# A post-norm decoder layer on one core: 1/std of the second and third layer norm from Ln and Exp on ScalarE and one refinement step on VectorE, in place of a bit-trick guess and three Newton steps on GpSimd

## What is computed

```
def _layernorm(x, axis=-1, eps=1e-05):
    m = jnp.mean(x, axis=axis, keepdims=True)
    v = jnp.var(x, axis=axis, keepdims=True)
    return (x - m) / jnp.sqrt(v + eps)

x = _layernorm(x + gelu((x @ ((w1 @ w2.T) * sparse_mask)) + b2))
x = _layernorm(x + cross_attention(x, ctx, ctx, mask, wq, wk, wv, wo))   # 32 query heads, 8 key heads, rope, softmax over 64 keys
x = _layernorm(x + x @ W.T + b + 2 * sum_e routing[b, e] * (x @ A_e.T) @ B_e.T)   # routing: softmax of the mean over tokens 107..254
```

## Time and profile before

| what | value |
|---|---|
| median of 3 runs | 492.2 us (491.89 to 492.32) |
| the profiled execution | 492.99 us, span 491.2 us |
| mean granted TensorE clock | 0.985 |
| busy share of the span | PE 96%, VectorE 83%, GpSimd 56%, ScalarE 53% |
| chain that ended last | PE 77%, VectorE 9%, the SP queue 4%, GpSimd 3%, issue 3%, DMA 2%, ScalarE 1% |

### The profile page before, as it was taken

One profiled execution on the slowest core, in us unless ns is written; L12 is line 12 of the kernel. 1 busy time (PEld: TensorE's weight loads), 2 busy tenths in 40 slices (PEclk: granted clock), 3 DMA queues, 4 the chain that ended last, 5 costly groups with the idle time before them and its releaser, 6 DMA issues.

```text
span 491.2 us, 11126 instructions
## 1 busy us (share of the span) xinstructions
PE 473.9 (96%) x4189; PEld 395.9 (81%) x4189; DVE 408.3 (83%) x739; ACT 260.6 (53%) x462; POOL 273.4 (56%) x347
## 2 busy tenths in 40 slices
PE   8999999999999999999999999999999999879991
PEld 8888778888888888888888888888888788668781
DVE  2779898988987898798979987988799889988585
ACT  4574447735673566365735663575458254353423
POOL 3477637854674467456636672676366423156523
PEclk9999999999999999999999999999999999979996
DMA  8943300240023011402040212022002400000013
GB/s 274 353 146 93 124 1 1 87 130 1 2 85 128 0 22 63 128 0 80 7 127 0 85 34 94 0 85 85 0 0 87 67 1 2 1 0 2 0 40 133
DMA packets 29137, 31.56 MB, mean 64 GB/s; under 512 B 6321, under 2 KB 16817, under 8 KB 29114
## 3 DMA queue, kind: packets, MB, share of 16 engines
q1 hardware_dynamic: 29114, 31.25, 20.1%
HBM read 29.15 MB, written 2.10 MB: 64 GB/s over the span
## 4 chain that ended last, share of the span: by engine, by line
PE 77%; DVE 9%; SPq 4%; POOL 3%; issue 3%; DMA 2%; ACT 1%; ACTq 0%; POOLq 0%; DVEq 0%
PE bank L261 23%; PE bank L263 22%; PE bank L262 22%; PE bank L369 6%; PE bank L393 3%; SPq L205 2%; DMA WQr<-in_L_xattn_wq_dram 2%; DVE X L1223 1%; DVE BST L1187 1%; PE bank L267 1%; POOL NW L1711 1%; DVE VWl L1139 1%; POOL NW L1709 1%; POOL RS L1713 1%; POOL NW L1707 1%
## 5 line engine op out<-in xcount | busy, mean ns | idle before, releaser
L1722 POOL TENSOR_TENSOR QS<-QS,SIN 128x512 f32<-128x512 f32 x64 | 83.0, 1297 | 124.4 <-ACT QS L801 124.4
L261 PE MATMUL bank<-XTh,WQh 128*128 128x512 f32 x256 | 101.7, 397 | 0.7 <-DVE XTl L1139 0.7
L263 PE MATMUL bank<-XTh,WQl 128*128 128x512 f32 x256 | 100.0, 391 | 0.0
L262 PE MATMUL bank<-XTl,WQh 128*128 128x512 f32 x256 | 99.7, 390 | 0.0
L1139 DVE TENSOR_TENSOR VWl<-bank,VWh 64x512 fp32r<-64x512 f32 x128 | 88.0, 688 | 9.3 <-ACT VWh L801 7.4
L801 ACT ACTIVATE QS<-bank 128x512 f32<-128x512 f32 x64 | 38.3, 598 | 103.1 <-PE bank L263 102.6
L801 ACT ACTIVATE VWh<-bank 64x512 fp32r<-64x512 f32 x128 | 75.9, 593 | 23.5 <-PE bank L263 20.9
L1251 DVE TENSOR_TENSOR bank<-bank,COS 128x512 f32<-128x512 f32 x64 | 44.6, 697 | 23.2 <-ACT QS L801 22.6
L261 PEld LDWEIGHTS bank<-XTh,WQh 128*128 128x128 f32 x256 | 48.1, 188 | 11.5 <-issue 1.3
L263 PEld LDWEIGHTS bank<-XTh,WQl 128*128 128x128 f32 x256 | 48.0, 188 | 10.5
L262 PEld LDWEIGHTS bank<-XTl,WQh 128*128 128x128 f32 x256 | 48.1, 188 | 9.5
(11 more groups left out here) (150 smaller groups left out, 965.1 us busy)
## 6 DMA issues: line engine op xcount, KB each, us to landing
WQr<-in_L_xattn_wq_dram SPq DMA_DIRECT2D x8, 1024.0 KB, 5.5
WOr<-in_L_xattn_wo_dram SPq DMA_DIRECT2D x8, 1024.0 KB, 5.4
KVr<-in_L_xattn_wk_dram SPq DMA_DIRECT2D x8, 256.0 KB, 5.4
KVr<-in_L_xattn_wv_dram SPq DMA_DIRECT2D x8, 256.0 KB, 5.5
out_dram<-X SPq DMA_DIRECT2D x8, 256.0 KB, 2.0
X<-in_x_dram SPq DMA_DIRECT2D x3, 512.0 KB, 9.9
WQr<-in_L_attn_w_dram SPq DMA_DIRECT2D x4, 256.0 KB, 4.9
WOr<-in_L_attn_w_dram SPq DMA_DIRECT2D x4, 256.0 KB, 5.1
```

The costliest lines, as they stand in the source:

```text
L261: pe.matmul(o, lh, rh, start=start, stop=False)
L262: pe.matmul(o, lh, rl, start=False, stop=False)
L263: return pe.matmul(o, ll, rh, start=False, stop=stop)
L1722: pool.tensor_tensor(q, q, SIN[:, :].unsqueeze(1).broadcast_to([P, 2, S]), ALU.mult)\
```

## The change

For layer norms 1 and 2, `guess`, `newton`, `mean_shift` and `out_last` are no longer called. In their place ScalarE's `std_first` writes Exp(-0.5 * Ln(var + eps)) of a pair, in two dependent activations on 128x2. VectorE's `std_step` then does one Newton step in three dependent fused instructions, and a fourth for minus mean times 1/std. The last pair goes the same way, with tile 6 written by VectorE (`out_by_dve`) as before. GpSimd sets the tile `EPS` once at the start and has no part in these two norms any more. Layer norm 0 is as it was.

With it, the written order of all four engines from group LAST on is another one, and so are some bank tables (`x2_bank`, `fy_bank`, `F_BANKS`, `LORA_BANKS`, `ROUTE_BANK`). The number of matmuls and the loop over the groups before LAST are the same.

```
+            def std_first(k, m):
+                pair, n = slice(2 * m, 2 * m + 2), 4 * (k - 1) + m
+                act.wait_ge(sm["ln_mean"], NT * k + 2 * m + 2)
+                act.wait_ge(sm["eps_set"], 1)
+                act.activation(RS[:, pair], MV[:, pair, 1], ACT.Ln, bias=EPS[:, 0:1]).then_inc(sm["ln_log"], 1)
+                act.wait_ge(sm["ln_log"], n + 1)
+                act.activation(RS[:, pair], RS[:, pair], ACT.Exp, scale=-0.5).then_inc(sm["ln_first"], 1)
...
             def normalize(k, t):
-                act.wait_ge(sm["ln_shift"], 2 * (t // 2 + 1))
+                act.wait_ge(sm["ln_step"], 4 * (t // 2 + 1))
...
+            def std_step(k, m):
+                pair, n = slice(2 * m, 2 * m + 2), 4 * (k - 1) + m
+                mean, var, r, w = MV[:, pair, 0], MV[:, pair, 1], RS[:, pair], NW[:, pair]
+                dve.wait_ge(sm["ln_first"], n + 1)
+                dve.scalar_tensor_tensor(out=w, in0=r, scalar=-0.5, in1=r, op0=ALU.mult, op1=ALU.mult).then_inc(sm["ln_step"], 1)
+                dve.wait_ge(sm["ln_step"], 4 * n + 1)
+                dve.scalar_tensor_tensor(out=w, in0=var, scalar=LN_EPS, in1=w, op0=ALU.add, op1=ALU.mult).then_inc(sm["ln_step"], 1)
+                dve.wait_ge(sm["ln_step"], 4 * n + 2)
+                dve.scalar_tensor_tensor(out=r, in0=w, scalar=1.5, in1=r, op0=ALU.add, op1=ALU.mult).then_inc(sm["ln_step"], 1)
+                dve.wait_ge(sm["ln_step"], 4 * n + 3)
+                dve.scalar_tensor_tensor(out=NM[:, pair], in0=mean, scalar=-1.0, in1=r, op0=ALU.mult, op1=ALU.mult)\
+                    .then_inc(sm["ln_step"], 1)
```

More of the change, by code:

```diff
@@ L647, in _ @@
             score_pair(LAST - 1, 3)
+            pe.wait_ge(sm["vw_lo"], n_vw(LAST - 1, 4))
+            value_out(LAST - 1, 6, 3)
             pe.wait_ge(sm["q_rot"], n_rot(LAST - 1, 3, 0))
@@ L651, in _ @@
             value_out(LAST - 1, 7, 7)
+            pe.wait_ge(sm["pt_lo"], n_unit(LAST - 1, 1))
+            attend(LAST - 1, 0)
             pe.wait_ge(sm["q_rot"], n_rot(LAST - 1, 3, 1))
             query(LAST, 0, 1)
-            pe.wait_ge(sm["pt_lo"], n_unit(LAST - 1, 1))
-            attend(LAST - 1, 0)
             pe.wait_ge(sm["vw_lo"], n_vw(LAST - 1, 6))
             attend(LAST - 1, 1)
+            pe.wait_ge(sm["vw_lo"], n_vw(LAST - 1, 7))
+            probs_transpose(LAST - 1, 2)
             pe.wait_ge(sm["x_added"], n_added(LAST - 1, 0))
@@ L661, in _ @@
             query(LAST, 1, 0)
[L662 to L663 removed]
             pe.wait_ge(sm["x_added"], n_added(LAST - 1, 2))
[L665 removed]
+            attend(LAST - 1, 3)
             pe.wait_ge(sm["s_sub"], n_unit(LAST - 1, 3))
             scores(LAST, 0)
+            pe.wait_ge(sm["x_added"], n_added(LAST - 1, 3))
+            probs_transpose(LAST - 1, 3)
             pe.wait_ge(sm["q_rot"], n_rot(LAST, 0, 1))
             query(LAST, 1, 1)
[L670 to L671 removed]
             pe.wait_ge(sm["pt_lo"], n_unit(LAST - 1, 3))
[L673 removed]
+            attend(LAST - 1, 4)
+            pe.wait_ge(sm["pt_lo"], n_unit(LAST - 1, 2))
+            value_out(LAST, 0, 7)
             pe.wait_ge(sm["q_rot"], n_rot(LAST, 0, 0))
@@ L677, in _ @@
             scores(LAST, 1)
-            pe.wait_ge(sm["pt_lo"], n_unit(LAST - 1, 2))
-            probs_transpose(LAST, 0)
+            pe.wait_ge(sm["x_added"], n_added(LAST - 1, 4))
+            attend(LAST - 1, 5)
             pe.wait_ge(sm["vw_lo"], n_vw(LAST, 0))
[L681 to L685, removed]
+            value_out(LAST, 1, 7)
@@ L686, in _ @@
+            pe.wait_ge(sm["q_rot"], n_rot(LAST, 1, 0))
+            weight_transpose(0)
             pe.wait_ge(sm["q_rot"], n_rot(LAST, 1, 1))
             query(LAST, 2, 1)
[L688 to L691, removed]
             pe.wait_ge(sm["vw_lo"], n_vw(LAST, 1))
+            probs_transpose(LAST, 0)
+            pe.wait_ge(sm["x_added"], n_added(LAST - 1, 1))
@@ L693, in _ @@
             attend(LAST - 1, 6)
             pe.wait_ge(sm["x_added"], n_added(LAST - 1, 5))
+            value_out(LAST, 2, 6)
+            pe.wait_ge(sm["pt_lo"], n_unit(LAST, 0))
+            value_out(LAST, 3, 7)
+            pe.wait_ge(sm["f_lo"], 1)
+            query(LAST, 3, 0)
+            pe.wait_ge(sm["vw_lo"], n_vw(LAST, 2))
             attend(LAST - 1, 7)
-            pe.wait_ge(sm["x_added"], n_added(LAST - 1, 6))
-            weight_transpose(0)
             pe.wait_ge(sm["s_sub"], n_unit(LAST, 1))
@@ L699, in _ @@
             scores(LAST, 2)
-            pe.wait_ge(sm["q_rot"], n_rot(LAST, 1, 0))
-            query(LAST, 3, 0)
             pe.wait_ge(sm["x_added"], n_added(LAST - 1, 7))
-            probs_transpose(LAST, 1)
-            pe.wait_ge(sm["f_lo"], 1)
-            value_out(LAST, 4, 3)
+            value_out(LAST, 4, 6)
+            pe.wait_ge(sm["x_added"], n_added(LAST - 1, 6))
+            value_out(LAST, 5, 3)
             pe.wait_ge(sm["q_rot"], n_rot(LAST, 2, 1))
             query(LAST, 3, 1)
+            pe.wait_ge(sm["vw_lo"], n_vw(LAST, 4))
@@ L708, in _ @@
+            probs_transpose(LAST, 1)
+            pe.wait_ge(sm["q_rot"], n_rot(LAST, 2, 0))
+            weight_transpose(1)
+            pe.wait_ge(sm["pt_lo"], n_unit(LAST, 1))
+            attend(LAST, 0)
+            pe.wait_ge(sm["s_sub"], n_unit(LAST, 2))
+            scores(LAST, 3)
+            pe.wait_ge(sm["vw_lo"], n_vw(LAST, 5))
+            attend(LAST, 1)
+            pe.wait_ge(sm["q_rot"], n_rot(LAST, 3, 1))
+            weight_transpose(2)
             pe.wait_ge(sm["vw_lo"], n_vw(LAST, 3))
@@ L709, in _ @@
             probs_transpose(LAST, 2)
[L710 to L715, removed]
             pe.wait_ge(sm["x_added"], n_added(LAST, 0))
             attend(LAST, 2)
-            pe.wait_ge(sm["s_sub"], n_unit(LAST, 2))
-            scores(LAST, 3)
+            pe.wait_ge(sm["x_added"], n_added(LAST, 1))
@@ L720, in _ @@
+            value_out(LAST, 6, 3)
+            pe.wait_ge(sm["pt_lo"], n_unit(LAST, 2))
+            value_out(LAST, 7, 7)
             pe.wait_ge(sm["x_added"], n_added(LAST, 2))
             attend(LAST, 3)
[L722 to L728, removed]
@@ L729, in _ @@
-            value_out(LAST, 7, 7)
             pe.wait_ge(sm["q_rot"], n_rot(LAST, 3, 0))
             weight_transpose(3)
+            pe.wait_ge(sm["f_lo"], 2)
+            weight_transpose(4)
             pe.wait_ge(sm["x_added"], n_added(LAST, 3))
             probs_transpose(LAST, 3)
-            pe.wait_ge(sm["s_sub"], n_unit(LAST, 3))
+            pe.wait_ge(sm["vw_lo"], n_vw(LAST, 6))
             x2_tile(0)
+            pe.wait_ge(sm["pt_lo"], n_unit(LAST, 3))
+            attend(LAST, 4)
@@ L736, in _ @@
+            pe.wait_ge(sm["f_lo"], 3)
+            weight_transpose(5)
+            pe.wait_ge(sm["f_lo"], 4)
+            weight_transpose(6)
             pe.wait_ge(sm["s_sub"], n_unit(LAST, 3))
             x2_tile(1)
[L738 to L743, removed]
             pe.wait_ge(sm["x_added"], n_added(LAST, 4))
             attend(LAST, 5)
-            pe.wait_ge(sm["vw_lo"], n_vw(LAST, 6))
+            pe.wait_ge(sm["tr_lo"], 19)
@@ L1548, in _ @@
             q_cos(LAST, 0, 0)
-            vw_lo(LAST - 1, 6, 3)
             pt_lo(LAST - 1, 1)
@@ L1841, in _ @@
             wo_lo(LAST, 2)
+            probs(LAST - 1, 2)
             wo_lo(LAST, 3)
             q_sin(LAST, 0, 1)
-            probs(LAST - 1, 2)
             probs(LAST - 1, 3)
@@ L1849, in _ @@
             q_sin(LAST, 2, 0)
+            probs(LAST, 1)
             q_sin(LAST, 2, 1)
-            probs(LAST, 1)
             q_sin(LAST, 3, 0)
+            q_sin(LAST, 3, 1)
             probs(LAST, 2)
-            q_sin(LAST, 3, 1)
-            newton(1, 0)
-            mean_shift(1, 0)
             probs(LAST, 3)
```

271 lines of the change are left out of this document (126 added, 145 removed).

## The result

The changed kernel takes 503.9 us (median of 4 runs, 503.2 to 505.6) against 492.3 before, run beside it: a ratio of 1.0237, interval 1.0216 to 1.0257. The profiled execution takes 503.2 us with a span of 501.4, 10.2 more than before.

A forecast was written before the change was run, and what follows sets the result against it. Bound by TensorE's waits and half-rate clock in the last group, and the chain behind the last matmul. +4.3 + 1.0 + 3.6 = +8.9 on the profiled 492.99 gives 501.9, less 0.8 to the median: 501.1 us, range 484.5 to 505.

The forecast's parts named there:

- Ln and Exp fetch a table in turn: In norms 1 and 2 each Ln and each Exp loads its own table, 16 loads for eight pairs; chance 0.60.
- A load's price of 1.3 or 2.6 per pair: At `std_first`, 1.3 us more where ScalarE arrives early and Ln's load is hidden, 2.6 more where it arrives late.
- the last group: Last group with loads: waits of 11.2 us against 6.9 us of old waits and clock loss, +4.3 us.
- the clock: Last group: long waits bring TensorE's clock down again, costing 1.0 us, bounds 0 and 2.9.
- Where it lands: TensorE waits 4.5 us before `x2_tile(0)`; pair 2 delays `x2_tile(4)` by 2.0, pair 3 `x2_tile(6)` by 3.0.
- The other small waits: Around the last unit: 1.0 us before `attend(LAST, 0)`, 0.5 before `scores(LAST, 3)`, 0.6 at `attend(LAST, 4)`, 0.4 in small ones.
- Behind the last matmul: From the last matmul to the span's end: -3.5 us without loads, +3.6 with them, ScalarE and VectorE alternating without slack.
- The sum without loads: Whole change without table loads: -2.5 us around the last unit and -3.5 behind the last matmul, -6.0 together.
- rival (a): Norms 1 and 2: the loads don't recur; 486.2 us, range 484 to 489; chance 0.22.
- GpSimd's steps in the way of the last unit's probabilities: `newton(1, 0)` and `mean_shift(1, 0)` ahead of `probs(LAST, 3)` make it late; without them TensorE's 2.3 us wait is gone.
- Rival (b): No recurring loads, but the new order wins nothing on TensorE, only the end gains: 489.1 us; chance 0.12.
- Rival (c): The loads recur but lie mostly in ScalarE's idle time: 490 to 493 us; chance 0.06.

The follow-up runs named there:

- the version with one table: The changed kernel with one table holding both Ln and Exp loaded ahead of the first Exp: 487.7 us, ratio 0.9909; measured again 487.9 us, 0.9901.
- the version with loads in the last pair: The version with one table, plus the table of Ln alone loaded ahead of the last pair: 489.8 us, ratio 0.9949 to the kernel before.

## Why the forecast held, step by step

- *Ln and Exp fetch a table in turn.* Right. This was the one step that no row of before could decide, and it was put at 0.60; the argument, that Gelu's table carries the copies and still wasn't chosen for them, pointed the right way. The runs show the outcome and not the rule by which a load picks its table: behind `natural_log` Exp fetched another table, behind `exp_and_others` Ln did, and behind the table with both neither did. The rule of the Trainium skill that ln followed by exp needs one load ("ScalarE: Activation LUTs", "Table sets: the hidden batching unit") does not hold for the loads as they were placed in this kernel, 16 for eight pairs; its statement that one set holds both is borne out by the version with one table, 3 loads in all.
- *A load's price of 1.3 or 2.6 per pair.* Right for the length (1.28 each) and for what it costs where ScalarE is late: 2.1 for the last pair. For the norms as a whole the forecast had 7.8 in the last group (6.8 and 1.0 for the clock) and 7.1 at the end (from -3.5 to +3.6); the runs have 9.2 and 6.8.
- *Where it lands.* `x2_tile(0)` 4.5 forecast, 3.80 measured; `x2_tile(4)` 2.0 and 3.01; `x2_tile(6)` 3.0 and 3.01. The last matmul was forecast 5.3 later (4.3 and 1.0 for the clock) and came 7.0 later. The 0.7 too much at `x2_tile(0)` is spent one step earlier: 0.65 stand ahead of `probs_transpose(LAST, 3)`, whose bank `accumulate(LAST, 3)` has to free first, and the forecast had walked the probabilities alone there. Of the 1.7 that was missed, `x2_tile(4)` is 1.0 and the clock, whose loss was 1.5 and not 1.0, is 0.5. The other small waits (1.35, 0.46 and 0.23, from 414 to 423) are 0.3 more than forecast for them (1.7, which is 2.5 less the 0.8 to be saved), and the kernel before had one of 0.28 at 424.76 that the forecast did not take off. That leaves 0.2 open.
- *Behind the last matmul.* +3.6 forecast, +3.2 measured; from the last mean and variance (493.90) to tile 7's start (497.84) 3.9, inside the 2.7 to 4.5 named. The rounds were right: from `std_step(2, 0)` to the end of the span 20.6 forecast and 20.7 measured (480.68 to 501.4). They began 7.4 ahead of the last matmul's end and not 6.8.
- *The sum without loads,* rival (a): 486.2 forecast, 487.7 and 487.9 measured. The last matmul at 478.5 forecast, 479.05; from the last mean and variance (0.18 from 480.53 on, so 480.71) to tile 7's start (482.10) 1.4 forecast and 1.4 measured; the wait before `x2_tile(0)` 1.9 forecast, 1.48. The clock held in the profiled executions, as assumed. The total is 1.5 and 1.7 above the forecast all the same. 0.8 of that is the step from the profiled execution to the median, which the forecast took over from the kernel before; the profiled executions took 487.45 and 487.91 against 492.99 - 6.0 = 487.0, so 0.5 and 0.9 are missed in the kernel itself.
- *GpSimd's steps in the way of the last unit's probabilities.* Right: with the order kept and the steps gone the wait fell by 0.94. The other 1.36 of the 2.30 are not theirs: `probs` itself takes 1.04 behind the row inverse. And the wait alone was not their price. They were late for the norm too, as the edit that only swaps them shows.
- *The total.* 501.1 forecast, 503.9 measured. The profiled executions differ by 10.2, the medians by 11.6; the forecast was 8.9. So 1.3 of the 2.8 that was missed lies in the kernel's terms, and the rest in the step from the profiled execution to the median: before it lay 0.8 above its median, after the change 0.7 below.

Rival (b), an order that wins nothing on TensorE, is refuted for the profiled executions of the version with one table: the last matmul ends 2.0 earlier than before. But it names what some executions do. Where the clock falls, as in the profile of the version with loads in the last pair, the last matmul ends at 480.82, 0.2 earlier than before, and one of the eight executions with one table took 489.2 at a mean clock of 0.992, where (b) says 489.1; that one was not profiled. Rival (c), loads hidden in ScalarE's idle time, is refuted by the total (490 to 493 forecast) and by the cost of the loads, 16.2 us for 20.5 us of them.

## What to carry to other kernels

Before a second curve function is brought into a kernel, find out which table each function fetches, and count the loads in the profile: here two dependent activations of 0.3 and 0.2 us cost 3.1 with their loads. Where one table holds all functions, load it by name at a place where a load stands anyway; here that one line turned a loss of 2.4% into a gain of 0.9%. And an engine's steps that are late in front of one consumer are not mended by moving them behind it if the next consumer follows at once: take them out or make them shorter.

## What the runs showed of the hardware that was not expected

- The same pattern of waits did not always bring the clock down. In the version with one table TensorE's timeline has 0.65 and 1.48 us idle before 434.06 and the clock stays at 1.00. In the profile of the version with loads in the last pair alone the same two waits, 0.65 and 1.48, are followed by 2 us and more at 0.50:

```profile
436.00:438.00 2.00, 2.00 (x8) 1.52 (x7) 1.09 (x4) 0.00 (x0) 0.34 (x1) 0.50 0.00 0
```

  From `x2_tile(0)` to `x2_tile(4)` that kernel takes 20.0 us (434.29 to 454.30) and the version with one table 18.5 (434.06 to 452.54), with the same program up to that place. The 1.5 is about the distance between the two groups of its runs (four at 489.7 to 489.8, two at 491.2 and 491.4). What decides is not settled.
- In the changed kernel the first instruction of `std_step` took 0.84 and 0.56 us at two of the eight pairs, against 0.16 at the others. These two started while GpSimd ran an `add_bias`, and each ended 0.02 behind it (453.13 and 453.11, 459.96 and 459.94):

```profile
452.29 0.84 DVE L1241 SCALAR_TENSOR_TENSOR NW<-RS 128x2 f32<-128x2 f32 x1 [2.34 <-ACT RS L932]
459.40 0.56 DVE L1241 SCALAR_TENSOR_TENSOR NW<-RS 128x2 f32<-128x2 f32 x1 [2.94 <-ACT RS L932]
```

```profile
451.85 1.26 POOL L1780 TENSOR_TENSOR X<-X,WOr 128x512 f32<-128x512 f32 x1 [1.91 <-PE bank L268]
458.68 1.26 POOL L1780 TENSOR_TENSOR X<-X,WOr 128x512 f32<-128x512 f32 x1 [1.91 <-PE bank L268]
```

  The same holds in all twelve traces, the kernel before included. In norms 1 and 2 they have 20 small VectorE instructions (128x2, the statistics not counted) that started inside an `add_bias`, more than 0.1 us ahead of its end; each took 0.37 to 1.18 us and ended 0.01 to 0.04 behind it. Full-width steps beside it keep their length: the statistics at 437.42 take 0.69 while an `add_bias` runs from 437.65 on. In the changed kernel the first of the two cost `x2_tile(4)` some 0.7 of the 1.0 us by which its wait was mis-sized. That GpSimd's instruction holds VectorE's is the reading of these rows; no run took `add_bias` away to test it.
